# Attention units turned in pairs, with the exponential four units ahead in place of six

## The reference

```
q = layernorm(x) @ wq ; k, v = ctx @ wk, ctx @ wv      # 16 query heads of 32, 2 key/value heads
q, k = rope(q), rope(k)
p = softmax(where(mask == 0, -1e9, q @ k.T / sqrt(32))) # 512 x 512 for each head and sequence
x = x + (p @ v) @ wo
x = x + experts(layernorm(x))                           # 8 experts, the best 2 of each token, and a shared one
```

## Time and profile before

| | |
|---|---|
| median of 3 runs | 1407.29 us (1404.77 to 1408.74) |
| the profiled execution | 1408.64 us, its span 1406.8 us |
| busy over the span | TensorE 95%, VectorE 68%, ScalarE 59%, GpSimd 41% |
| busy from 320 to 420 us | TensorE 97.6, VectorE 89.1, ScalarE 89.0, GpSimd 41.3 of 100 us |
| granted TensorE clock | 0.984 of full speed over the span |

### The profile page before, as it was taken

How to read it: one execution, slowest core, us unless ns; L and a number is a source line. 1 busy time by engine, 2 the same in 40 slices (tenths; PEclk the granted TensorE clock), 3 DMA queues, 4 the chain that set the end, 5 groups by cost and what they waited for, 6 DMA issues and landing times.

```text
span 1406.8 us, 28203 instructions
## 1 busy us (share of the span) xinstructions
PE 1339.5 (95%) x8061; PEld 1025.5 (73%) x8061; DVE 959.3 (68%) x2665; ACT 836.6 (59%) x1951; POOL 581.3 (41%) x724
## 2 busy tenths in 40 slices
PE   6898999999999999999898999999999999999997
PEld 4675776767767677676565777777778888888885
DVE  6888989888897888988776666666653433334332
ACT  2788979889798897988983222222213333334332
POOL 3443433434344253342254333333343555555553
PEclk9799999999999999999999999999999999999999
DMA  6545464564644646545366232222257879786552
GB/s 205 149 134 152 130 193 144 144 200 136 193 144 134 201 138 181 153 139 162 104 199 216 73 101 85 82 89 84 76 174 183 216 160 279 193 196 106 111 77 37
DMA packets 145780, 206.53 MB, mean 147 GB/s; under 512 B 35295, under 2 KB 72799, under 8 KB 145634
## 3 DMA queue, kind: packets, MB, share of 16 engines
q1 hardware_dynamic: 124274, 166.84, 38.7%
q0 software_dynamic: 17952, 33.64, 12.7%
q10 hardware_dynamic: 3408, 4.26, 0.9%
HBM read 105.42 MB, written 69.35 MB: 124 GB/s over the span
## 4 chain that ended last, share of the span: by engine, by line
PE 73%; ACT 11%; DVE 5%; issue 3%; DMA 3%; POOL 3%; SPq 2%; DVEq 0%; POOLq 0%; ACTq 0%
PE psum L1505 13%; PE psum L1507 13%; PE psum L1506 13%; PE psum L695 7%; PE psum L810 6%; ACT a_probs L593 6%; PE psum L789 6%; ACT a_probsT L599 3%; PE psum L740 3%; PE psum L742 3%; PE psum L741 3%; PE psum L1572 1%; PE psum L1601 1%; PE psum L710 1%; DVE a_probs L957 1%
## 5 line engine op out<-in xcount | busy, mean ns | idle before, releaser
L593 ACT ACTIVATE a_probs<-a_probs,a_low 128x512 f32<-128x512 f32 x512 | 366.4, 716 | 82.3 <-DVE a_low L957 82.0
L957 DVE CUSTOM_DVE_ANT_0 a_probs<-psum,a_bias 128x512 f32<-128x512 f32 x512 | 343.7, 685 | 70.3 <-PE psum L789 66.9
L695 PEld LDWEIGHTS psum<-a_ident_r,a_probs_bits 128*128 128x128 f32 x2048 | 225.8, 142 | 88.1 <-issue 28.2
L695 PE MATMUL psum<-a_ident_r,a_probs_bits 128*128 128x128 f32 x2048 | 247.1, 245 | 14.9 <-ACT a_probsT L599 8.6
L789 PE MATMUL psum<-a_kT,a_q_stack 128*128 128x512 f32 x512 | 245.7, 481 | 13.4 <-DVE a_low L957 7.7
L599 ACT ACTIVATE a_probsT<-psum 128x512 f32<-128x512 f32 x328 | 189.9, 580 | 5.4 <-PE psum L695 4.7
L1374 POOL DMA_INDIRECT out<-b_y,b_pairs_sb x71 | 112.6, 1586 | 149.8 <-DMA out<-b_y,b_pairs_sb 79.8
L963 DVE COPY a_probsT<-psum 128x512 f32<-128x512 f32 x184 | 126.0, 685 | 2.8 <-PE psum L695 1.7
L1807 DVE SCALAR_TENSOR_TENSOR b_v_hidden<-b_v_hidden,psum 128x256 f32<-128x256 f32 x71 | 29.9, 421 | 134.3 <-ACT b_v_hidden L1470 89.5
L810 PE MATMUL psum<-a_probsT,a_v 128*32 128x512 f32 x1024 | 117.7, 600 | 0.0
L1505 PE MATMUL psum<-b_w,b_vT_hi 128*128 x284 | 116.6, 410 | 0.0
(11 more groups left out here) (221 smaller groups left out, 2973.1 us busy)
## 6 DMA issues: line engine op xcount, KB each, us to landing
b_w<-w_halves SPq DMA_DIRECT2D x16, 1536.0 KB
a_q_stack<-a_qT_hi SPq DMA_DIRECT2D x254, 64.0 KB, 2.0
a_q_stack<-a_qT_lo SPq DMA_DIRECT2D x253, 64.0 KB, 2.0
w_halves<-a_w_hi SPq DMA_DIRECT2D x96, 128.0 KB, 2.0
w_halves<-a_w_lo SPq DMA_DIRECT2D x96, 128.0 KB, 1.9
a_xT_in<-in_x_turned SPq DMA_DIRECT2D x32, 256.0 KB, 2.9
a_ctx_in<-in_ctx SPq DMA_DIRECT2D x32, 256.0 KB, 3.0
a_x_in<-in_x SPq DMA_DIRECT2D x32, 256.0 KB, 3.2
```

What stands on the lines that cost most here:

```text
L593: nc.scalar.activation(probs[:, h % 2, t], probs[:, h % 2, t], ACT.Exp, bias=low[:, h % H, t:t + 1], scale=-1.0, accum_out=total[:, h // G ...
L695: last = nc.tensor.transpose(out[:, P * i:P * (i + 1)].bitcast(F32R), src(i), ident_r[:])
L957: nc.vector.tensor_tensor_reduce(probs[:, h % 2, t], psum[:, t % 2], bias[:, t], 1.0, HUGE, ALU.add, ALU.min, low[:, h % H, t:t + 1]).then ...
```

## The change

ScalarE's loop does exp(u+4) in place of exp(u+6). VectorE's loop and the score matmuls stay six ahead. TensorE goes through the units in pairs: T(u), T(u+1), then all small turns (`kT`, `qT`, `inverse`) that stand at u or u+1, then S(u+6), the rest of u, S(u+7), the rest of u+1. The ring's list takes the same new order. In `start`, the first two exponentials of head 1 are left out, since the loop now reaches them itself. The tables of what stands beside a unit are as before.

```
-AHEAD = 6
+AHEAD, EXP_AHEAD = 6, 4
...
+    TURNED = ("kT", "qT", "inverse")
+
+    def beside_pair(u):
+
+        first, second = PE_AT.get(u, ()), PE_AT.get(u + 1, ())
+        turns = [p for p in first + second if p[0] in TURNED]
+        return turns, [p for p in first if p[0] not in TURNED], [p for p in second if p[0] not in TURNED]
+
     line = []
-    for u in range(H * TT):
-        line.append(("probs", u))
-        line += [(kind, i) for kind, i in PE_AT.get(u, ()) if kind in RINGED]
+    for u in range(0, H * TT, 2):
+        turns, first, second = beside_pair(u)
+        line += [("probs", u), ("probs", u + 1)]
+        line += [(kind, i) for kind, i in turns + first + second if kind in RINGED]
...
                     exp(b, H, t)
-                exp(b, H + 1, 0)
-                exp(b, H + 1, 1)
                 turned_q(part, b, HG + 1)
...
-                if u + AHEAD < H * TT or part != "last":
-                    exp(b, (u + AHEAD) // TT, u % TT ^ 2)
+                if u + EXP_AHEAD < H * TT or part != "last":
+                    exp(b, (u + EXP_AHEAD) // TT, u % TT)
...
-            for u in range(H * TT):
-                turn_probs(part, b, u // TT, u % TT)
-                if u + AHEAD < H * TT or part != "last":
-                    scores(b, par, (u + AHEAD) // TT, u % TT ^ 2)
-                beside(part, b, par, u)
+            for u in range(0, H * TT, 2):
+                turns, first, second = beside_pair(u)
+                for w in (u, u + 1):
+                    turn_probs(part, b, w // TT, w % TT)
+                beside(part, b, par, u, turns)
+                for w, others in ((u, first), (u + 1, second)):
+                    if w + AHEAD < H * TT or part != "last":
+                        scores(b, par, (w + AHEAD) // TT, w % TT ^ 2)
+                    beside(part, b, par, w, others)
```

More of the change, by code:

```diff
@@ L813, in weighted, with beside @@
                 last.then_inc(s["out_filled"], 1)
-        def beside(part, b, par, u):
-            for kind, i in stages(part, PE_AT, u):
+        def beside(part, b, par, u, places):
+            for kind, i in places:
+                if not there(part, kind, i):
+                    continue
                 if kind == "kv":
```

## The result

| | before | after |
|---|---|---|
| median of 4 runs each, in turn | 1408.01 us (1404.77 to 1411.92) | 1427.28 us (1425.56 to 1428.83) |
| ratio | | 1.0138, 95% interval 1.0118 to 1.0158 |
| span of the profiled execution | 1406.8 us | 1424.1 us, granted clock 0.988 |

The changed kernel is 1.4% slower. The forecast was 1404, in a range of 1385 to 1417: wrong in sign, and outside the range.

A forecast was written before the change was run, and what follows sets the result against it. TensorE, nearly full, was taken as the bound. Middle bodies -3.1 us, clock +3.4 and outer bodies -5 took 1408.6 to 1403.9, forecast 1404 us; own range 1399 to 1409, 8 in 10 from 1385 to 1417.

The forecast's parts named there:

- units 0 and 1: Start of a middle body: T(0) and T(1) stop waiting for ring banks, gaining 0.29 + 0.53 = 0.8 us.
- some 0.9 us further there: Last quarter of a middle body: without waits for low(), ScalarE gets this far ahead.
- the waits at 24, 28 and 29 (0.9 together) should go: Second quarter: these TensorE waits vanish because ScalarE resumes earlier behind the W.
- kT 1: Moved ahead of S(40) and S(41), it loses 0.53 us where late; its wait grows to 2.0 to 2.7 us.
- Eight in a row: TensorE's paired transposes: 1.18 us a pair in place of 1.20, gaining 0.6 us a body, 0.3 behind kT 1.
- ScalarE's waits for low() under 20: Sign the forecast is right: ScalarE's idle time on low() over six bodies falls from 57 us to below 20.
- First quarter: S(8) comes about 0.35 us later, W of unit 17 0.15 to 0.3 later; loss 0.15 us a body.
- Clock: Middle bodies, after kT 1's longer waits: three half-clock stretches in place of one, costing +3.4 us.
- The rival of the transposes: Behind the W's, transposes let the clock fall: four half-clock stretches a body, +41 us, 1449 us; chance 0.04.
- First and last body: Fewer ScalarE waits for low() in the two outer bodies: gains of 2 us and 3 us.
- The rival in which the exponential becomes the wait: Transposes wait 0.37 us for exponentials at six places, 2.8 us a body: 1428 us, or 1417 with half lead; chance 0.14.

The follow-up runs named there:

- e10: The changed kernel with the evacuation of unit 27 on VectorE and that of unit 25 on ScalarE in exchange: 1.0146 of the kernel before.
- e1: The kernel before with only ScalarE's exponential four units ahead in place of six, TensorE's order unchanged: ratio 0.9974, 1407.5 us.
- e3: The changed kernel with the small turns back behind S(u+6) of their own unit; pairs and exponential four ahead stay: 1.0062 of the kernel before, 1419.1 us.
- e12: The changed kernel with the four kT turns back behind S(u+6) of their own unit, qT and inverse still behind the eight: 1.0086 of the kernel before.
- e6: The changed kernel with two ScalarE copies, spread 0 and xT 3, moved later, behind the evacuation of unit 27: 1.0152 of the kernel before.
- e7: The changed kernel with the last output piece (wo 15) and VectorE's add 3 one unit earlier, at 61: 1.0149 of the kernel before.
- e11: The kernel before with the exponential five units ahead in place of six: ratio 1.0010.
- e8: The kernel before with the exponential four ahead and VectorE's inverse 0 at unit 14 in place of 15: ratio 0.9953, 1405.1 us.

## Why the prediction was wrong

**The step that failed** is in the second quarter and in the part on units 0 and 1: that ScalarE "is some 0.9 us further there", that this "covers both waits at units 0 and 1", and that "the waits at 24, 28 and 29 (0.9 together) should go, since ScalarE resumes earlier". I gave the exponential's lead to the pairs as if their ring were the old one. It is not. In a pair every small turn and both scores stand behind T(u+1), so a small operation beside the first unit needs a bank that was filled one unit later than before, and T(u) and T(u+1) hand over two banks at once, which at units 26 and 27 one engine empties one after the other, with an exponential and more between. A lead of 0.9 doesn't cover that: the copy of unit 27 starts 3.6 us behind its transposes. And there was no lead: the 49 us that ScalarE no longer waits for low() came back as waits for transposes (4.0 to 53.7 us over the six middle bodies). The waits at 24 to 29, 0.9 in all, did not go: one of 1.61 stands there, and e10 shows whose bank it is. The second quarter was to be 0.9 shorter and is 1.62 longer; the fourth, with the 0.8 of units 0 and 1, is 0.34 longer. By e1, e3 and after, pairs cost 0.9% where I had -0.02 us a pair, and the small turns 0.76% where I had "nothing" but kT 1's 0.53.

Point by point:

- Eight in a row: 0.63 to 0.65 us from start to start, as in the earlier trace rows, then 0.30 between the two scores and 0.23 behind the second, as counted. The gain of 0.6 a body is hardly to be seen in the sum.
- ScalarE's waits for low() under 20: right, 7.4. T(1)'s ring wait is gone, and in e1 most of T(0)'s too. But in after T(0) waits for VectorE's last residual sum, which I had not looked at:

```profile
405.22 0.40 PE L796 MATMUL psum<-a_kT,a_q_stack 128*128 128x512 f32 x1
406.24 0.89 PE L702 MATMUL psum<-a_ident_r,a_probs_bits 128*128 128x128 f32 x8 [0.62 <-DVE a_x_res L1004]
```

- First quarter: W of unit 17 no sooner, right; 0.60 later, where I had 0.15. The step (S(8) behind both transposes) was the right one, and mis-sized: VectorE waits for each late score anew (62.0 us in place of 45.7 over the middle bodies), and TensorE in turn for VectorE, at units 5, 17 and 19 to 23, not once.
- kT 1: the mechanism is right. e12, which puts back all four `kT`, has a third quarter 0.67 us shorter, for the 0.53 forecast. Its wait is 1.21 in place of the 2.0 to 2.7 forecast, mostly since the 0.9 of removed waits that were to be given back there were never won.
- Clock: three half-clock stretches forecast in the middle bodies, none came, so the term of +3.4 us was wrong there; waits of up to 1.4 us at kT 1 left the clock at 1.00. The one behind kT 1 came in the first body, where a wait of 0.70 followed the one of 1.34. The rival of the transposes, with four stretches a body, did not come either: with eight and more in a row the middle bodies stayed at 1.00 for 550 us. The rule of the Trainium skill, "TensorE: Matmul & The Clock Gate", Part 4 (PE-mode transpose), that transposes don't count as busy in the same way for the clock gate, could have let it fall behind them; nothing of it shows in these bodies.
- First and last body: -2 and -3 forecast; +1.4 and -2.7 measured in the profile, by luck near the forecast in the last. From the W of unit 17 to the end of the first body after takes 69.4 us; e6 and e7, which have no half-clock stretch there, take 67.2 and 66.9, and before 66.6. In the last body before has 6.8 us at half clock and after none. e1, with as much at half clock in its last body as before, has -2.0 and -3.6: these shares were right for the exponential, and in the first body the pairs took it.
- The rival in which the exponential becomes the wait: its 2.8 us a body has no working (six places of 0.37 are 2.2), and what shows of it is 0.27. That its 1428 was met is luck.
- The collision was not in the prediction at all: about 1 us of the second quarter, in e1 as in after, given back in the first when it is mended.

Of the sum, the middle body was to be -0.5 and is +3.4. By the profiled bodies: the exponential +0.28 (collision included), pairs +1.96, small turns +1.16.

**What stays open.** Within the pairs' 1.96 us the late scores and the younger ring banks are not told apart: no run gives the one without the other. That they are one loop is argued from e6 and e7, and not shown. The small turns' part points to the scores: in e3 and e12 kT 0's wait is nearly what it was (1.3 for 1.6), and the time still comes back. And what follows the last W takes 669.5 us in e1 and 670.3 in e11 for 663.9 before, with a wait for the residual of 3.8 us in e1 and 5.6 in e11 (1.2 before) and a half-clock stretch of 6.8 us at 751 in both; e8 has 663.8. It hides part of e1's and e11's gain in their profiles, and I have not found why it comes.

## What to carry over

Before a transpose or a turn is moved in a ring of banks, write down for each entry which bank it will need and who empties it: an entry that stands behind its neighbour, and used to stand ahead of it, needs a bank one place younger, and the time that this takes must be found on the queue of the engine that empties it. An engine that stops waiting for its input is ahead only if it isn't then waiting for its other input; read both waits before a lead is spent. Where mending one wait after another leaves the time as it is, suspect the order itself: here the smaller edit alone, the exponential four ahead, is the faster kernel.

## What the hardware did that I had not expected

VectorE's operation of 128x16 on two SBUF inputs took 1.21 us instead of 0.17 while GpSimd ran its operations of 1.28 and 1.29 us on two SBUF inputs; the cast ahead of it, with one SBUF input, took 0.67 instead of 0.17, and up to 1.18 elsewhere. GpSimd's own took no longer than before (1.28 and 1.29). The Trainium skill, "GPSIMD Engine Reference", Specifications, says that the SBUF interfaces are shared with VectorE and names two cases of contention: VectorE's instructions with two SBUF inputs, and those in a 2-port mode. The trace agrees for the first; whether the cast was in such a mode no run here shows. The trace also shows what it is worth here: the small operation is not slowed in proportion, it ends when GpSimd's does (both at 154.6, the cast and the operation beside it at 153.3).
